# GpSimd adds the attention result behind the first normalisation and the last stage's tanh product

## The reference

```python
x = x + _L0_xattn_ref(ctx, ctx, _layernorm(x), ssm_kernel, D, 8)     # long convolution of products of ctx
x = x + _L0_ffn_ref(_layernorm(x), ...)                             # bit-linear gate * value, quantised
x = x + _L1_xattn_ref(_layernorm(x), ctx, mask, mask, ...)          # attention with 16 heads of 8
x = x + _L1_ffn_ref(_layernorm(x), ...)                             # top 32 of 512 genes by logits
```

## Time and profile before

| what | value |
|---|---|
| median of 3 runs | 624.97 us (624.21 to 626.88) |
| profiled execution, span | 623.6 us |
| TensorE busy | 491.8 us (79%) |
| VectorE busy | 478.8 us (77%) |
| GpSimd busy | 400.9 us (64%) |
| ScalarE busy | 346.5 us (56%) |
| costliest group of VectorE | line 1503, 128 reductions of 1216 ns, 155.6 us |
| the two instructions of the attention sum | 16 each, 729 and 727 ns |
| the product with the tanh | waits for ScalarE 10 times, 29.8 us in all |

### The profile page before, as it was taken

One profiled execution on the slowest core, in us unless ns is written; L12 is line 12 of the kernel. 1 busy time (PEld: TensorE's weight loads), 2 busy tenths in 40 slices (PEclk: granted clock), 3 DMA queues, 4 the chain that ended last, 5 costly groups with the idle time before them and its releaser, 6 DMA issues.

```text
span 623.6 us, 11640 instructions
## 1 busy us (share of the span) xinstructions
PE 491.8 (79%) x3633; PEld 280.0 (45%) x3633; DVE 478.8 (77%) x885; ACT 346.5 (56%) x578; POOL 400.9 (64%) x711
## 2 busy tenths in 40 slices
PE   1575888899796787979988988899987977887543
PEld 1464657666573343444444444444433433332221
DVE  4564658888889777899999999999978768784451
ACT  1246632313213475767877877778856657676431
POOL 6687487888897476677787787685654553422341
PEclk9888879999999798989999999999979879988875
DMA  6950100120235255544563465454464455411100
GB/s 195 371 114 7 29 17 2 26 44 0 75 42 125 52 97 127 115 82 110 95 122 102 86 142 109 78 140 96 95 145 98 86 130 104 87 29 39 46 8 17
DMA packets 92178, 54.31 MB, mean 87 GB/s; under 512 B 14851, under 2 KB 91844, under 8 KB 92118
## 3 DMA queue, kind: packets, MB, share of 16 engines
q1 hardware_dynamic: 92118, 53.58, 38.6%
HBM read 35.64 MB, written 17.42 MB: 85 GB/s over the span
## 4 chain that ended last, share of the span: by engine, by line
issue 20%; DVE 19%; PE 19%; DVEq 17%; POOL 15%; POOLq 7%; ACT 1%; ACTq 0%
PE pair L273 4%; PE bank L490 4%; POOL kv L888 4%; DVE w_int L1503 4%; DVEq L1544 3%; DVEq L1461 3%; DVEq L1554 3%; POOL yT L845 2%; DVEq L1412 2%; DVE prod L1365 2%; DVE best L1555 2%; DVEq L1515 2%; DVE st L1413 2%; DVEq L1440 2%; PE pair L461 2%
## 5 line engine op out<-in xcount | busy, mean ns | idle before, releaser
L1503 DVE TENSOR_REDUCE w_int<-pair 128x4 f32<-128x1024 f32 x128 | 155.6, 1216 | 23.0 <-PE pair L461 22.8
L1227 ACT ACTIVATE cT<-pair 128x1024 f32<-128x1024 f32 x128 | 130.9, 1023 | 62.1 <-PE pair L477 60.3
L273 PE MATMUL pair<-kv,toep 128*128 128x256 f32 x384 | 103.8, 411 | 27.9 <-POOL kv L888 10.6
L273 PEld LDWEIGHTS pair<-kv,toep 128*128 128x128 f32 x384 | 74.5, 205 | 48.3 <-issue 27.9
L888 POOL TENSOR_TENSOR kv<-cT 128x512 f32<-128x512 f32 x64 | 66.1, 1041 | 22.0 <-PE pair L273 15.9
L461 PE MATMUL pair<-KS,w_raw 54*128 54x256 bf16 x512 | 52.5, 285 | 30.0 <-DVE w_int L1503 29.9
L490 PE MATMUL bank<-cT,v_aug 128*32 128x256 f32 x1024 | 74.4, 411 | 0.0
L477 PE MATMUL pair<-w_raw,KS 57*128 57x256 bf16 x512 | 52.8, 287 | 15.8 <-DMA w_raw<-w_int 7.7
L1365 DVE TENSOR_TENSOR prod<-pair,qT 128x512 f32<-128x512 f32 x64 | 44.2, 691 | 24.8 <-PE pair L273 20.6
L461 PEld LDWEIGHTS pair<-KS,w_raw 54*128 54x128 bf16 x512 | 16.4, 97 | 73.2 <-DVE w_int L1503 58.7
L1372 DVE TENSOR_REDUCE yT<-prod 128x64 f32<-128x512 f32 x64 | 43.9, 686 | 6.2 <-issue 0.4
(11 more groups left out here) (163 smaller groups left out, 1013.6 us busy)
## 6 DMA issues: line engine op xcount, KB each, us to landing
w_raw<-scr_q SPq DMA_DIRECT2D x32, 192.0 KB
KS<-scr_k SPq DMA_DIRECT2D x32, 192.0 KB
scr_q<-w_int SPq DMA_DIRECT2D x16, 192.0 KB, 2.6
scr_k<-w_int SPq DMA_DIRECT2D x16, 192.0 KB, 2.6
scr_o<-qT SPq DMA_DIRECT2D x64, 36.0 KB
yT<-in_x SPq DMA_DIRECT2D x4, 512.0 KB, 7.5
ctx_all<-in_ctx SPq DMA_DIRECT2D x4, 512.0 KB, 7.9
x_b<-in_x SPq DMA_DIRECT2D x16, 128.0 KB, 5.2
```

The lines of the kernel that those rows point to most:

```text
L273: mm = pe.matmul(bank[:, lh * n:(lh + 1) * n], toep[:, h, (lh - sh) * P:(lh - sh + 1) * P], rhs[:, sh, :], start=(sh == 0), stop=(sh == lh))
L1227: act.activation(probs[g % 4].rearrange("p j l -> p (j l)"), SC[:], ACT.Exp).then_inc(s("scores_free"), 1)
L1503: dve.tensor_reduce(neg_max[:, :, 2 * g:2 * g + 2].rearrange("p t j -> p j t"), M[:].rearrange("p (j t s) -> p j t s", t=KL, s=L), AX.X, A ...
```

## The change

`add_attention(m - 9)` leaves its place in front of `normalise_x1(m)` and goes behind `down_times_xr(m - 11)`. The steps themselves, their waits and their signals stay as they are, and no other engine's list changes.

```diff
@@ -1064,9 +1064,9 @@
                 later_products(m - 2, 6)
                 later_products(m - 2, 7)
                 split_qk(m - 5)
-                add_attention(m - 9)
                 normalise_x1(m)
                 down_times_xr(m - 11)
+                add_attention(m - 9)
                 later_products(m - 2, 8)
                 normalise_x3(m - 9)
                 split_maxima(m - 7)
```

## The result

| kernel | median | span of the profiled run |
|---|---|---|
| before | 624.8 us | 623.6 us |
| changed | 675.5 us | 672.1 us |

The ratio is 1.080, with a 95% interval of 1.076 to 1.084. The change costs 50.7 us, where 37.5 us had been forecast. All medians here are over every run of a kernel, while the ratios, and their 95% intervals, leave out single runs that took over 1.5% longer than the fastest of the same kernel and so aren't exactly the quotients of the medians.

What follows compares the result with a forecast made beforehand. VectorE's full queue was taken to bound the middle, TensorE behind the third normalisation the tail. Span 623.6 + 29.5 (stalls) + 8.0 (clock) = 661.1 us, plus 1.4 us gives a median of 662.5 us, 6.0% slower; range 650 to 674 us.

Steps and rivals of the forecast that it cites:

- What bounds the kernel: VectorE's queue is full in the middle (250 to 430 us); in the tail TensorE's work waits behind the third normalisation.
- The stall: VectorE waits at the third statistics for the later x3, some 2.2 us in most iterations from 11 on; 29.5 us in all.
- the first rival: TensorE's clock stays up behind the new pauses, so only the stalls count: 654.5 us; chance 0.27.
- The second one: Tanh early enough for GpSimd's product, so statistics barely late: 4 us, 629 us; chance 0.03 together with the fourth rival.
- the earlier normalisation: Third rival: first normalisation 1.6 us earlier in seven iterations (9 to 15), up to 11 us faster, 614 us; chance 0.03.
- the price of the clock drops: TensorE at the lower clock behind new pauses, nearly each of 12 iterations, 1.75 us lost per drop; 8.0 us counted.
- the other eight: Iterations with a drop where VectorE leads and hides most of the 1.75 us: 0.35 us each.
- the four others: Iterations 19 to 22, where TensorE leads behind the normalisation: 1.3 us of the 1.75 us counted for each drop.
- upper bound of 21 us: Clock term if all 12 iterations lose the full 1.75 us of TensorE's time; the lower bound was 0.

Runs made afterwards that it cites:

- The two halves of the change: Sum moved behind the product only in iterations 9 to 17 (656.3 us), or only from 18 on (648.35 us), against 626.4 us for the kernel before.

## Why the prediction was wrong, point by point

**What bounds the kernel: right.** VectorE's full queue in the middle and TensorE behind the third normalisation in the tail are what the stalls hit. The two halves of the change cost 29.9 and 21.9 us, each more than its stalls alone.

**The stall: right in place and size.** From the start of the product to that of the statistics 2.38 us were summed, 2.38 us were measured in m = 14. The stall of the iterations like m = 14 was forecast as 2.20 us and is 2.28 us; in m = 20 it was 2.12 us and is 2.20 us:

```profile
551.04 0.74 POOL L1037 TENSOR_TENSOR toep<-qT 128x256 f32<-128x256 f32 x1 [3.71 <-ACT qT L1286]
...
553.43 0.43 DVE L1413 BATCH_NORM_STATS2 st<-qT 128x6 f32<-128x256 f32 x1 [2.20 <-POOL qT L1015]
...
555.28 0.39 PE L461 MATMUL pair<-KS,w_raw 54*128 54x256 bf16 x4 [2.83 <-DVE w_int L1503]
```

The twelve waits of iterations 11 to 22 are 26.9 us against 26.0 us. That all 13 waits come to 29.6 us, against a forecast sum of 29.5 us, is luck in part. The thirteenth is that of iteration 9, 2.7 us where 1.0 was forecast (1.15 us in the run with the spare matmuls). Iteration 23 isn't among them: it was forecast as 2.4 us, and VectorE waits 8.2 us there, against 3.2 us before. With the clock held up in the middle the kernel took 655.7 us; the first rival, "the clock holds", said 654.5 us.

**The other rivals.** The second one (the tanh doesn't hold the product up) was given as 629 us; with the wait taken out it is 627.3 us. Nothing became faster by the earlier normalisation: with the sum behind it alone the kernel is 0.3% slower.

**The step that failed is the price of the clock drops.** That there would be one in nearly each of the 12 iterations was right: there is one in each, behind pauses forecast as 2.8 to 2.9 us and measured as 2.83 and 2.96 us, with a mean clock of 0.93 in the middle, as forecast. Their length was nearly right too: 12 x 3.5 = 42 us at the lower level in the prediction, 48 us in the trace. What was wrong is the share that was taken to be hidden. "In the other eight VectorE leads and hides most: 0.35 us", and the 1.3 us for the four others, made 8.0 us of what is about 20 us, nearly the upper bound of 21 us.

The trace with spare matmuls gives the price by iteration. From the statistics of iteration 11 to those of 22 the changed kernel takes 297.5 us and the one with spare matmuls 278.2 us. Of these 19.3 us, 8.6 lie in the six steps of the middle (1.0 to 1.6 us each, and 2.2 us behind the statistics of m = 14), where 0.35 us had been taken, and 10.7 in the five steps behind them (1.6 to 2.9 us), where the 1.3 us had been taken for four. The second number holds a little of what the spare matmuls won from the tail's older drops. 624.8 + 29.5 + 20 = 674 us.

Two rows of the kernel before show the reserve that was counted on (order of time, m = 14):

```profile
379.82 0.39 PE L461 MATMUL pair<-KS,w_raw 54*128 54x256 bf16 x4
...
381.39 1.22 DVE L1503 TENSOR_REDUCE w_int<-pair 128x4 f32<-128x1024 f32 x1
```

TensorE's product was ready at 380.2, some 1.2 us before VectorE's reduction took it. With the drop of 6.8 us in m = 14, the work from product to product takes 6.33 instead of 3.72 us, 2.6 us more. 2.6 less 1.2 is 1.4 us, which is the 1.44 us that VectorE waits. With a drop of 3.4 us, the common case, that reserve is nearly enough. In m = 13 of the changed kernel:

```profile
362.65 0.61 PE L461 MATMUL pair<-KS,w_raw 54*128 54x256 bf16 x4 [2.96 <-DVE w_int L1503]
...
367.70 0.39 PE L461 MATMUL pair<-KS,w_raw 54*128 54x256 bf16 x4
...
368.20 1.23 DVE L1503 TENSOR_REDUCE w_int<-pair 128x4 f32<-128x1024 f32 x1 [0.17 <-PE pair L461]
...
371.15 1.23 DVE L1503 TENSOR_REDUCE w_int<-pair 128x4 f32<-128x1024 f32 x1 [0.30 <-PE pair L461]
```

From product to product it is 5.05 us, 1.3 us more. Against the kernel with spare matmuls, the first reduction is 0.25 us late. At the next hand-over the reserve was smaller in the kernel before (the product ready at 383.2, the reduction at 383.95: 0.7 us), and there the delay becomes 0.64 us, the 1.3 less the 0.7 us. The step to the 1.0 us that this iteration loses lies at line 1516 of VectorE, which takes 0.96 instead of 0.59 us; in both traces it ends within 0.05 us of GpSimd's line 965. Why that one ends later was not tested. So the reserve of an engine that isn't the bound was there, but the smallest reserve in the row decides, and the drop falls right behind the stall, on a dense stretch of TensorE's work.

The range ended at 674 us, just under what the prediction's own upper bound of the term gives: 625.0 + 29.5 + 21 = 675.5 us. With both bounds written down (0 and 21 us), the upper one should have been inside.

## What to carry to other kernels

Ahead of a move in a strict queue, list what the steps that one moves past wait for: the move past a 1.9 us normalisation cost 0.3%, the move past a 0.7 us product that waits for another engine cost 8%. A stall has a second price where it gives TensorE a pause: look for what TensorE does directly behind the pause, compare its length at the lower clock with the reserve before each of the next hand-overs, and count as hidden only what the smallest of them covers. And look for all waits on the signal that becomes late: the ring buffer of an earlier stage may wait for it as well.

## What the runs showed of the hardware

The clock's price has a step in it. TensorE's pause of 2.29 us in each iteration brought the same loss of about 20 us as one of 2.96 us, so cutting the stall by a third gave back 10 of 50.7 us, the stall's own share and none of the clock's. In the middle of the kernel, pauses of 0.75 and 0.94 us had no drop behind them, those of 1.10 to 1.38 us two in five, and those from 1.94 us on one each. Which drops last 3.4 and which 6.8 us differs between executions with the same pause. Eighteen spare matmuls of 128 x 256 in the pause, 2.14 us of work that nobody reads, held the clock at the upper level in the middle and made the kernel 19.8 us faster.

The same remedy in the kernel before took 28 us at the lower level out of the tail and won only 2.7 us. Half of a stretch at the lower level is TensorE's time lost; of that half, the drops of 3.4 us in the middle cost the changed kernel 1.0 to 1.6 of 1.7 us, and those of the old tail, with the spare matmuls' own cost in it, 2.7 of 14 us. What is paid depends on what the slow stretch falls on.
